# Row gathers issued without a bound on their row numbers

## The reference

```python
x = x + gnn(layernorm(x), adj, W, a)       # graph attention over 1024 tokens, then elu
x = x + ffn(layernorm(x), Wq_pk, pk_keys, Wq, keys_table, values_table, Wo)

# in ffn, for each token and each of 8 heads:
scores, idx = top_k(sim, 16)                        # for two halves, 128 keys each
score = scores[0][..., :, None] + scores[1][..., None, :]
final_scores, pk_idx = top_k(score, 16)             # 16 of 256 sums
ind = indices + head * 16384                        # 16 row numbers below 131072
k = einsum('bnhk,bnhkd->bnhd', softmax(final_scores), keys_table[ind])
v = einsum('bnhk,bnhkd->bnhd', softmax(final_scores), values_table[ind])
out = causal_attention(q, k, v) @ Wo
```

## Time and profile before

| | |
|---|---|
| median of 3 runs | 11159.58 us (11158.63 to 11160.57) |
| profiled execution, first to last instruction | 11164.0 us |
| POOL busy | 77% |
| DVE busy | 61% |
| PE busy | 51% |
| ACT busy | 28% |
| DMA engines busy, mean | about a third |

### The profile page before, as it was taken

How to read it: one execution, slowest core, us unless ns; L and a number is a source line. 1 busy time by engine, 2 the same in 40 slices (tenths; PEclk the granted TensorE clock), 3 DMA queues, 4 the chain that set the end, 5 groups by cost and what they waited for, 6 DMA issues and landing times.

```text
span 11164.0 us, 115118 instructions
## 1 busy us (share of the span) xinstructions
PE 5689.6 (51%) x23108; PEld 4344.2 (39%) x23108; DVE 6812.2 (61%) x26972; ACT 3111.6 (28%) x9770; POOL 8574.0 (77%) x8209
## 2 busy tenths in 40 slices
PE   5545554554555545555555554555545445545444
PEld 3433343333433334333343333433334333333333
DVE  7766666666656666666666666666656666655553
ACT  3322232222222222222222222322222222222222
POOL 6777777777777777777777777777777777777777
PEclk7777777777777777777777777777777777777777
DMA  3333333333333333333333333333333333333333
GB/s 103 94 98 98 97 101 98 97 97 97 101 97 97 97 97 101 97 97 97 97 101 97 97 97 101 98 97 97 97 101 98 98 97 97 98 99 97 98 98 93
DMA packets 413967, 1092.49 MB, mean 98 GB/s; under 512 B 132480, under 2 KB 150144, under 8 KB 413440
## 3 DMA queue, kind: packets, MB, share of 16 engines
q0 software_dynamic: 393216, 1074.27, 33.4%
q1 hardware_dynamic: 20352, 14.82, 0.4%
HBM read 1084.36 MB, written 4.19 MB: 98 GB/s over the span
## 4 chain that ended last, share of the span: by engine, by line
POOL 75%; issue 21%; POOLq 2%; DVE 1%; PE 1%; DMA 0%; ACT 0%; SPq 0%; DVEq 0%
POOL ring L276 75%; POOLq L276 2%; PE ps_w L547 0%; DMA wo<-in_Wo 0%; POOLq L292 0%; DVE idx L881 0%; POOLq L290 0%; DMA ring<-in_table,idx 0%; PE ps_o L597 0%; PE ps_s L619 0%; DVE hot L873 0%; POOLq L291 0%; POOLq L288 0%; PE ps_p L486 0%; DVE sidx L820 0%
## 5 line engine op out<-in xcount | busy, mean ns | idle before, releaser
L276 POOL DMA_INDIRECT ring<-in_table,idx x8192 | 8571.6, 1046 | 2564.8 <-issue 2494.7
L547 PE MATMUL ps_w<-ring,diag 128*128 128x256 f32 x8192 | 3073.9, 556 | 4595.4 <-DMA ring<-in_table,idx 4589.1
L547 PEld LDWEIGHTS ps_w<-ring,diag 128*128 128x128 f32 x8192 | 2361.0, 296 | 5208.2 <-issue 4561.4
L791 DVE TENSOR_SCALAR ps_v<-ring,wgt 128x256 f32<-128x256 f32 x512 | 249.1, 486 | 2200.1 <-DMA ring<-in_table,idx 2199.0
L794 DVE SCALAR_TENSOR_TENSOR ps_v<-ring,wgt,ps_v 128x256 f32<-128x256 f32 x3072 | 1475.7, 480 | 19.6
L381 ACT COPY probT<-ps_p 128x512 f32<-128x512 f32 (+3 forms) x768 | 342.7, 481 | 3792.8 <-PE ps_p L591 3792.8
L367 ACT ACTIVATE diag<-ident,wgt 128x128 f32<-128x128 f32 x4096 | 1251.5, 390 | 1.8 <-PE ps_w L547 1.8
L881 DVE TENSOR_REDUCE idx<-hot 128x16 uint32<-128x864 f32 x512 | 828.7, 1618 | 0.0
L597 PE MATMUL ps_o<-probT,kv 128*128 128x128 f32 x4608 | 663.5, 290 | 320.1 <-ACT probT L381 320.1
L597 PEld LDWEIGHTS ps_o<-probT,kv 128*128 128x128 f32 x4608 | 564.7, 195 | 447.8 <-ACT probT L381 432.7
L376 ACT ACTIVATE prob<-ps_s,nmax 128x128 f32<-128x128 f32 (+7 forms) x512 | 380.1, 742 | 1096.0 <-DVE nmax L916 1096.0
(11 more groups left out here) (119 smaller groups left out, 7647.1 us busy)
## 6 DMA issues: line engine op xcount, KB each, us to landing
ring<-in_table,idx POOLq DMA_INDIRECT x8192
xin<-in_x SPq DMA_DIRECT2D x8, 512.0 KB, 4.3
mask<-in_adj SPq DMA_DIRECT2D x1, 4096.0 KB, 14.5
out_x<-acc SPq DMA_DIRECT2D x64, 64.0 KB, 2.4
ring<-in_WqpkT SPq DMA_DIRECT2D x1, 512.0 KB, 16.6
ring<-in_keysT SPq DMA_DIRECT2D x1, 512.0 KB, 18.3
wq<-in_Wq SPq DMA_DIRECT2D x1, 512.0 KB, 18.7
wo<-in_Wo SPq DMA_DIRECT2D x1, 512.0 KB, 19.7
```

The source lines that it names most:

```text
L276: pool.indirect_dma_start(out=ring[:, t % RING, k, :], out_offset=None, in_=table, in_offset=bass.IndirectOffsetOnAxis(ap=idx[:, t, k:k + ...
L547: ins = nc.tensor.matmul(pw_ps, diag[:, k, :], ring[:, t % RING, k, :], start=(k == 0), stop=(k == PE_ROWS - 1))
```

## The change

The call that issues a gather loses two arguments: the bound, which is the number of the last row of the table, and the setting that a row number above it is an error. In the program that is built, the bound is a register operand of the gather, and a register MOVE ahead of every gather writes the constant 131071 into it. The changed program has neither the operand nor the MOVE: of GpSimd's 259 MOVEs in the program's text (gathers in the loop's body counted once) 3 are left, and a gather that carried its waits through the MOVE now carries them itself. The number of gathers, their order, their sizes, the waits at the head of each unit and the values of the waits are the same. No other engine's instructions differ.

```diff
                 for k in range(TOPK):
                     pool.indirect_dma_start(
                         out=ring[:, t % RING, k, :], out_offset=None, in_=table,
-                        in_offset=bass.IndirectOffsetOnAxis(ap=idx[:, t, k:k + 1], axis=0),
-                        bounds_check=HEADS * NUM_KV - 1, oob_is_err=True).then_inc(rows_dma[t], 16)
+                        in_offset=bass.IndirectOffsetOnAxis(ap=idx[:, t, k:k + 1], axis=0)).then_inc(rows_dma[t], 16)
```

## The result

The changed kernel takes 10593.28 us (median of 4 runs, 10591.91 to 10595.09) against 11160.08 us for the kernel before in the same measurement. The ratio is 0.949, with a 95% interval of 0.948 to 0.950: 5.1% faster. The forecast was 11,160 us, the range 10,900 to 11,240.

What follows compares the result with a forecast made beforehand. GpSimd's serial gathers were taken to bound the kernel: 59.6 + 8571.6 + 2494.7 + 13.6 us plus a 24.5 us tail make 11164.0. Off the median 11159.6, both parts at 0 gave 11,160 us, range 10,900 to 11,240.

Steps and rivals of the forecast that it cites:

- What bounds the kernel: On GpSimd, 8192 gathers run one behind the other and set the end; one ns in a cycle is 8.19 us.
- Part 1: The 8192 MOVEs of 29 ns ahead of the gathers go; claimed worth nothing, gaps staying at 305 ns.
- the MOVE in series: Rival: the MOVE in the gap before each gather counts after all, 237.6 us, 10,922 us; chance 0.05.
- Part 2: The gather itself (line 276) without its bound; claimed to save 0 ns, the median staying at 1012 ns.
- The bounds, 0 to 192 ns: Limits on the check's price per gather: nothing if a comparison is always made, 192 ns at 1.5 ns a step.
- the nearest row is the gather's own: Reason for taking 0 ns: the gather's minimum and median, 1007 and 1012 ns, lie within 5 ns for fresh row numbers.
- row by row: Rival: a check for each row, or branches for groups, goes: 80 to 192 ns a gather, 10,504 to 9,590 us; chance 0.10.
- a few steps for many rows: Rival: a check of about ten steps in each gather goes: 12 ns, 98 us, 11,061 us; 4 to 20 ns counts; chance 0.30.
- The MEMSET and AFFINE_SELECT slopes: GpSimd rows for list work, 0.8 and 1.5 ns a step, used to price a check of 128 rows at 102 to 192 ns.
- The estimate from the Trainium skill: In each gather, eight branches for sixteen rows each, from about 12 cycles a branch: 80 ns, 655 us, time 10,504 us.
- The slower rival: Gathers overlapping DVE stretch half as much again: 17 ns a gather, +140 us, 11,299 us; chance 0.13, including unseen ways.
- The note on the SBUF page: DVE instructions with two SBUF inputs hold up GpSimd's reads; descriptor generation, which writes, is inferred to be left alone.

## Why the prediction was wrong

- **What bounds the kernel: right.** The end is a sum over 8192 gathers, before and after, and one ns in a gather's cycle was worth 8.19 us as forecast.
- **Part 1, the MOVEs cost nothing: right.** The gap stayed at 305 ns; writing the register once gave 1.000, two sequencer instructions more in each gap gave the changed kernel's time. The rival "the MOVE in series" (0.05, 10,922 us) is refuted twice.
- **Part 2, the gather without the bound: wrong, and it is the step that failed.** Its term was taken as 0 ns and measures 66 ns, 541 us of the 577.8 that the gathers lost (the other 37 are smaller stretch). The bounds, 0 to 192 ns, did hold it. What failed is the choice between them: "the nearest row is the gather's own", whose duration does not move with the data. That a duration is steady says that the work doesn't depend on the data; it says nothing on how much of this work is the check. The sentence picked the lower end without a row that bore on it, and the chances followed: 0.10 for 80 to 192 ns, 0.30 for 4 to 20 ns, and nothing at all for 20 to 80, where the answer lay. The range then stopped at 10,900 us, which was the MOVE's 29 ns, a price that part 1 had just thrown out.
- **The picture of the check was wrong too.** Both forms that I priced, row by row and a few steps for many rows, grow with the rows. The measured price is 53 ns at 64 rows and 55 at 32, and 13 of the 66 are for the error report alone. It is mostly a price that a gather with a bound pays whatever its rows from 32 to 64. The MEMSET and AFFINE_SELECT slopes price something that grows with the rows, and can't give it. Whether the price is for something done once a gather, or for rows compared side by side, isn't shown here.
- **The estimate from the Trainium skill** (GPSIMD Engine Reference, section 3.1: 80 ns for eight branches, 10,504 us) came nearest in size, 66 ns and 10,593 us, but its mechanism, one branch for each sixteen rows, would have halved the difference at 64 rows, and it did not: 53 ns are left there. The step before it, that the trace excludes a branch for each row, takes all 128 rows one after the other; no row of this case shows that they are handled so.
- **The slower rival, more stretch: refuted in its sign.** The stretch went from 34 to 30 ns a gather. Its place was right: the earlier trace rows named `hot`. Counted from the trace, gathers more than 20 ns above the median, each put down to the DVE operation that overlapped it most, `hot` stretches 324 gathers before (148 us) and 461 after (216 us), while `is_at` goes from 410 (68 us) to 22 (8 us). That shorter gathers meet the two operations at other moments would explain it and isn't tested. The sum of the two hardly changed; what fell by 40 us, and gave the 34 to 30 ns, is the part of the graph layer's operations on `edge`, 49 us before and 9 after.
- **The note on the SBUF page** (the Trainium skill, SBUF — State Buffer, "Who interferes with whom") was borne out in its first half: with one operand in SBUF instead of two, DVE stopped holding up gathers, 26 ns a gather down to 2 on one chip. A gather does read its row numbers from SBUF, so its inference that the writing of descriptors is left alone is neither borne out nor refuted: no run shows which part of a gather was held up. What is shown is that a gather as a whole isn't left alone.

## What to carry to other kernels

Where GpSimd's gathers set the time, leave out a bound that the data cannot exceed: 66 ns of 1012 here, 13 of them for the error report, and little of it would be saved by gathering fewer rows. What a gather without a bound does with a row number beyond the table no run here shows, so the bound may go only where the numbers are limited by how they are made. A register move or two semaphore increments ahead of a gather cost nothing here, where the sequencer was ahead; see whether the gap changes where a gap holds none of them. And where long DVE operations on two SBUF operands stretch the gathers, put the smaller operand in PSUM: 24 ns a gather here, paid with 0.4 us more of DVE for each `is_at`. When a cost is bounded from both sides and no row lies near it, spread the chances over the whole bracket.

## Hardware behaviour that was not expected

- A gather's time hardly follows its rows: without a bound 862 ns for 32, 899 for 64, 946 for 128, and 305 ns between two gathers with nothing, a MOVE or two semaphore increments in between.
- The option to report an out-of-bound row costs 13 ns in every gather even if none is out of bound.
- One chip, at one time, ran the kernel before in 13,482 us instead of 11,175. The trace of the version with bound and lists in PSUM, taken on it then, has idle times of up to 35 us before a gather that nothing in the profile explains, while a gather's median stayed at 1012 ns.
